# Causal attention on one Trainium2 core: transposes one step later, other score banks, maxima in two parts

## The reference

```python
def _temporal_experts(xt, idx, qw, qb, kw, kb, vw, vb, pw, pb):
    q = (jnp.einsum('btd,bod->bto', xt, qw[idx]) + qb[idx][:, None, :]).reshape(B, T, H, HD)
    k = ...
    v = ...
    logits = jnp.einsum('bthd,bshd->bhts', q, k) * HD ** (-0.5)
    causal = jnp.tril(jnp.ones((T, T), dtype=bool))
    logits = jnp.where(causal, logits, -jnp.inf)
    att = jax.nn.softmax(logits, axis=-1)
    o = jnp.einsum('bhts,bshd->bthd', att, v).reshape(B, T, D)
```

## Time and profile before

| what | us |
|---|---|
| median of 3 runs | 3260.94 (3252.55 to 3263.05) |
| the profiled execution's own time | 3263.12 |
| its span, first to last instruction | 3261.4 |
| the units of the causal attention, first to last exponential | 1883.96 to 2117.31 |
| TensorE busy in the span | 2921.0 |
| VectorE busy | 2001.2 |
| ScalarE busy | 1520.2 |

### The profile page before, as it was taken

One profiled execution on the slowest core, in us unless ns is written; L12 is line 12 of the kernel. 1 busy time (PEld: TensorE's weight loads), 2 busy tenths in 40 slices (PEclk: granted clock), 3 DMA queues, 4 the chain that ended last, 5 costly groups with the idle time before them and its releaser, 6 DMA issues. The chain is left out here.

```text
span 3261.4 us, 48231 instructions
## 1 busy us (share of the span) xinstructions
PE 2921.0 (90%) x15718; PEld 2067.5 (63%) x15718; DVE 2001.2 (61%) x4063; ACT 1520.2 (47%) x3320; POOL 945.4 (29%) x994
## 2 busy tenths in 40 slices
PE   5988699999689968799997989889999899998899
PEld 2622187776557645355555856568777687776787
DVE  6888736776521136799995256644777447776444
ACT  2500035666135526577774355524666346664322
POOL 2067573671134430677760000000000000001210
PEclk9999999999689989899998999999999999999999
DMA  3057755332669954555431653146220263201422
GB/s 98 17 166 203 200 151 131 64 66 50 178 226 335 336 154 148 184 147 161 147 106 42 199 131 82 25 135 171 60 56 22 64 190 80 59 22 40 113 78 84
DMA packets 227364, 401.31 MB, mean 123 GB/s; under 512 B 44750, under 2 KB 141154, under 8 KB 224942
## 3 DMA queue, kind: packets, MB, share of 16 engines
q1 hardware_dynamic: 176066, 260.74, 28.3%
q0 software_dynamic: 49744, 134.92, 14.9%
q10 hardware_dynamic: 1308, 2.56, 0.3%
HBM read 314.40 MB, written 87.71 MB: 123 GB/s over the span
## 5 line engine op out<-in xcount | busy, mean ns | idle before, releaser
L905 ACT ACTIVATE at_p<-at_pb,at_max 125x1250 f32<-125x1250 f32 (+4 forms) x320 | 383.8, 1199 | 301.9 <-DVE at_unused L976 273.3
L791 PE MATMUL at_pb<-ident,at_p 125*125 125x125 f32 x2880 | 431.9, 280 | 20.5 <-ACT at_p L905 17.7
L791 PEld LDWEIGHTS at_pb<-ident,at_p 125*125 125x125 f32 x2880 | 389.3, 190 | 83.3 <-ACT at_p L905 22.1
L808 PE MATMUL at_pb<-at_pt,at_v 125*64 125x250 f32 x2880 | 355.3, 383 | 5.2 <-DVE s_t L1009 3.0
L969 DVE TENSOR_REDUCE at_wide<-at_pb 125x1 f32<-125x1024 f32 x240 | 293.6, 1223 | 20.3 <-PE at_pb L774 2.0
L891 ACT ACTIVATE at_pt<-at_pb 125x500 f32<-125x500 f32 (+1 forms) x448 | 232.8, 520 | 94.8 <-PE at_pb L791 90.4
L808 PEld LDWEIGHTS at_pb<-at_pt,at_v 125*64 125x64 f32 x2880 | 188.4, 137 | 103.9 <-issue 14.3
L751 PE MATMUL at_pb<-at_s,at_shared 128*128 128x500 f32 (+1 forms) x1152 | 229.0, 361 | 22.9 <-ACT at_shared L853 22.9
L987 DVE COPY at_pt<-at_pb 125x500 f32<-125x500 f32 (+1 forms) x416 | 232.1, 582 | 21.9 <-PE at_pb L791 21.9
L976 DVE TENSOR_SCALAR_CACHE_REDUCE at_unused<-at_pb,at_wide 125x226 bf16<-125x226 f32 x240 | 107.7, 449 | 205.2 <-PE at_pb L774 202.3
L713 POOL TENSOR_TENSOR s_t<-s_t,at_all 128x500 f32<-128x500 f32 (+1 forms) x33 | 42.8, 1296 | 651.5 <-DVE s_t L1009 651.4
(11 more groups left out here) (340 smaller groups left out, 5694.1 us busy)
## 6 DMA issues: line engine op xcount, KB each, us to landing
w_ring<-in_L_ffn_w SPq DMA_DIRECT2D x128, 512.0 KB, 12.4
at_shared<-k_parts SPq DMA_DIRECT2D x64, 312.5 KB
ml_w<-in_mlp_w SPq DMA_DIRECT2D x64, 256.0 KB
k_parts<-at_shared SPq DMA_DIRECT2D x64, 250.0 KB, 2.8
q_parts<-at_shared SPq DMA_DIRECT2D x64, 250.0 KB, 2.8
h_edges<-em_both SPq DMA_DIRECT2D x44, 256.0 KB, 2.3
g_h<-h_edges SPq DMA_DIRECT2D x10, 1024.0 KB, 6.0
at_shared<-q_parts SPq DMA_DIRECT2D x32, 312.5 KB
```

The source lines that it names most:

```text
L791: ins = pe.transpose(pturn[0:TN, g % 2, TN * (t % 4):TN * (t % 4) + TN], p[:, u % 2, TN * t:TN * t + TN], c.ident[0:TN, 0:TN])
L808: ins = pe.matmul(pout[side:side + 64, 0:2 * TN], v[:, t, 2 * j + h, :], p_t[:, q % 2, t, :], start=(t < 2), stop=(t >= keys[u] - 2))
L905: act.activation(p[:, t % 2, 0:w], score[t % 2][0:TN, 0:w], ACT.Exp, bias=neg_max[:, t:t + 1], accum_out=total[:, t:t + 1]).then_inc(exp_d ...
```

## The change

Only the causal attention changes; the other three keep their instructions and order.

- `lag`: transposes and takes of a unit move from step u+2 to step u+3. TensorE's step s now is turns(s-3) parts 0 and 1, then scores(s), the quarters of duo (s-5)//2, and part 2 of the turns among them; a duo of up to 4 key tiles is done in one go. The lower half's copy and the addition move from odd step 2q+5 to even step 2q+6. The loops run one step longer.
- `place` and `spans`: units of fewer than 10 key tiles ("short") write their scores to banks of their own, even units to the first banks (`score[0]`), odd units to `apart`, the fourth and fifth bank, both in pieces that begin at column 0.
- The wait of a piece for the exponential of the unit before is left only in the third piece, where this unit and the one before are both full.
- Full units take the maximum in two parts. Even: `wide_max` over columns 0 to 1000, then `tail_max` masks 250 columns and takes the maximum over these. Odd: `wide_max` masks its last 125 columns and takes 1024, then `tail_max` takes the other 226.

```diff
--- before.py
+++ after.py
@@ -595,10 +595,16 @@
         keys = [(i // 2 * 2 + 2 if causal else NT) for _, _, i in units]
         turns = [-(-n // 4) for n in keys]
         upto = lambda u: sum(turns[:u])
+        full = lambda u: keys[u] == NT
+        wides = [u for u in range(NU) if causal and full(u)]
+        apart = flat[:, 3 * 512:5 * 512]
+        place = lambda u: apart if causal and u % 2 and not full(u) else score[u % 2]
+        spans = lambda u: pieces[0] if causal and not full(u) else pieces[u % 2]
+        lag = 3 if causal else 2
 
         taken = [(u, n) for u in range(NU) for n in range(turns[u])]
         by_act = lambda u, n: (n == 0 or (n == 2 and u % 2 == 0)) if causal else (n == 2) == (u % 2 == 0)
-        sum_at = lambda s: (s - 5) // 2 if causal and s % 2 == 1 else (s - 6) // 2 if not causal and s % 2 == 0 else -1
+        sum_at = lambda s: (s - 6) // 2 if s % 2 == 0 else -1
         act_by = lambda g: sum(1 for u, n in taken[:g] if by_act(u, n))
         dve_by = lambda g: g - act_by(g)
 
@@ -759,23 +765,23 @@
                     if u % UNITS == 0 and n == 0 and j >= 1:
                         pe.wait_ge(kq_in[j % 2], 16 * LOADS * ((j + 1) // 2))
                     w = TN * keys[u]
-                    there = [(a, min(b, w)) for a, b in pieces[u % 2] if a < w]
+                    there = [(a, min(b, w)) for a, b in spans(u) if a < w]
                     if n >= len(there):
                         return
                     a, b = there[n]
                     if u >= 2 and n == 0:
 
                         pe.wait_ge(exp_done, u - 1)
-                    if u >= 1 and a == (0 if u % 2 else 1024):
+                    if u >= 1 and full(u) and full(u - 1) and n == 2:
 
                         pe.wait_ge(exp_done, u)
-                    pe.matmul(score[u % 2][0:TN, a:b], q_two[j % 2][h][:, TN * i:TN * i + TN], k_hi[j % 2][h][:, a:b],
+                    pe.matmul(place(u)[0:TN, a:b], q_two[j % 2][h][:, TN * i:TN * i + TN], k_hi[j % 2][h][:, a:b],
                               start=True, stop=False)
-                    ins = pe.matmul(score[u % 2][0:TN, a:b], q_two[j % 2][h][:, TN * i:TN * i + TN], k_lo[j % 2][h][:, a:b],
+                    ins = pe.matmul(place(u)[0:TN, a:b], q_two[j % 2][h][:, TN * i:TN * i + TN], k_lo[j % 2][h][:, a:b],
                                     start=False, stop=True)
                     if n == len(there) - 1:
                         ins.then_inc(scored, 1)
-                    elif n == 1 and not causal:
+                    elif n == 1:
                         ins.then_inc(wide_scored, 1)
 
                 def turn_part(u, n):
@@ -812,19 +818,28 @@
 
                 pe.wait_ge(first_in, 16 * LOADS)
                 pe.wait_ge(low, len(items) - 3)
-                for s in range(NU + 4):
+                for s in range(NU + 5 if causal else NU + 4):
                     if s == 2:
 
                         pe.wait_ge(low, len(items))
                     if causal:
-                        quarter = 2 * (s % 2)
-                        turn_part(s - 2, 0)
+                        q, at = (s - 5) // 2, 2 * ((s - 5) % 2)
+                        short = 0 <= q < NU // 2 and keys[2 * q] <= 4
+                        wide = s < NU and full(s)
+                        turn_part(s - lag, 0)
+                        turn_part(s - lag, 1)
                         score_part(s, 0)
-                        turn_part(s - 2, 1)
-                        duo_sum((s - 4) // 2, quarter, quarter + 1)
-                        score_part(s, 1)
-                        turn_part(s - 2, 2)
-                        duo_sum((s - 4) // 2, quarter + 1, quarter + 2)
+                        if wide:
+                            score_part(s, 1)
+                        if not short:
+                            duo_sum(q, at, at + 1)
+                        turn_part(s - lag, 2)
+                        if not wide:
+                            score_part(s, 1)
+                        if not short:
+                            duo_sum(q, at + 1, at + 2)
+                        elif at == 0:
+                            duo_sum(q, 0, 4)
                         score_part(s, 2)
                     elif s % 2 == 0:
                         turn_part(s - 2, 0)
@@ -893,8 +908,8 @@
                                    ACT.Copy).then_inc(act_took, 1)
 
                 act.wait_ge(w_low, len(parts))
-                for s in range(NU + 4 if causal else NU + 5):
-                    take_part(s - 2, 0)
+                for s in range(NU + 5):
+                    take_part(s - lag, 0)
                     if 1 <= s <= NU:
                         t = s - 1
                         act.wait_ge(max_ready, t + 1)
@@ -902,10 +917,10 @@
 
                             act.wait_ge(turned, upto(t - 1))
                         w = TN * keys[t]
-                        act.activation(p[:, t % 2, 0:w], score[t % 2][0:TN, 0:w], ACT.Exp,
+                        act.activation(p[:, t % 2, 0:w], place(t)[0:TN, 0:w], ACT.Exp,
                                        bias=neg_max[:, t:t + 1], accum_out=total[:, t:t + 1]).then_inc(exp_done, 1)
-                    take_part(s - 2, 1)
-                    take_part(s - 2, 2)
+                    take_part(s - lag, 1)
+                    take_part(s - lag, 2)
                     if sum_at(s) >= 0:
                         q = sum_at(s)
                         act.wait_ge(pv_done, q + 1)
@@ -953,27 +968,44 @@
 
                 if save is not None:
                     dve.wait_ge(saved, 16)
+                def mask(u):
+                    w, m = TN * keys[u], TN * (2 - u % 2)
+                    late = place(u)[0:TN, w - m:w]
+                    dve.tensor_tensor(late, late, c.causal[:, 0:m], ALU.add).then_inc(masked, 1)
+                    dve.wait_ge(masked, u + 1)
+
                 def whole_max(u):
                     w = TN * keys[u]
                     dve.wait_ge(scored, u + 1)
-                    m = TN * (2 - u % 2)
-                    late = score[u % 2][0:TN, w - m:w]
-                    dve.tensor_tensor(late, late, c.causal[:, 0:m], ALU.add).then_inc(masked, 1)
-                    dve.wait_ge(masked, u + 1)
-                    dve.tensor_reduce(neg_max[:, u:u + 1], score[u % 2][0:TN, 0:w], AX, ALU.max, negate=True)\
+                    mask(u)
+                    dve.tensor_reduce(neg_max[:, u:u + 1], place(u)[0:TN, 0:w], AX, ALU.max, negate=True)\
                         .then_inc(max_ready, 1)
 
                 def wide_max(u):
                     a = pieces[u % 2][0][0]
-                    dve.wait_ge(wide_scored, u + 1)
-                    dve.tensor_reduce(neg_wide[:, u:u + 1], score[u % 2][0:TN, a:a + 1024], AX, ALU.max, negate=True)\
+                    b = a + 1024
+                    if causal:
+                        dve.wait_ge(wide_scored, wides.index(u) + 1)
+                        if u % 2:
+                            mask(u)
+                        else:
+                            b = N - 2 * TN
+                    else:
+                        dve.wait_ge(wide_scored, u + 1)
+                    dve.tensor_reduce(neg_wide[:, u:u + 1], score[u % 2][0:TN, a:b], AX, ALU.max, negate=True)\
                         .then_inc(wide_ready, 1)
 
                 def tail_max(u):
-                    a = pieces[u % 2][2][0]
+                    a, b = pieces[u % 2][2]
                     dve.wait_ge(scored, u + 1)
-                    dve.wait_ge(wide_ready, u + 1)
-                    dve.tensor_scalar(unused[:, 0:TAIL], score[u % 2][0:TN, a:a + TAIL], -1.0, neg_wide[:, u:u + 1],
+                    if causal:
+                        dve.wait_ge(wide_ready, wides.index(u) + 1)
+                        if u % 2 == 0:
+                            mask(u)
+                            a = N - 2 * TN
+                    else:
+                        dve.wait_ge(wide_ready, u + 1)
+                    dve.tensor_scalar(unused[:, 0:b - a], score[u % 2][0:TN, a:b], -1.0, neg_wide[:, u:u + 1],
                                       ALU.mult, ALU.min, accum_out=neg_max[:, u:u + 1]).then_inc(max_ready, 1)
 
                 def take_part(u, n):
@@ -987,13 +1019,13 @@
                     dve.tensor_copy(p_t[:, u // 2 % 2, 4 * n:4 * n + m, TN * (u % 2):TN * (u % 2) + TN],
                                     pturn[0:TN, g % 2, 0:TN * m].rearrange("p (a b) -> p a b", b=TN)).then_inc(dve_took, 1)
 
-                for s in range(NU + 4 if causal else NU + 5):
+                for s in range(NU + 5):
                     if 1 <= s <= NU:
-                        (whole_max if causal else tail_max)(s - 1)
-                    u = s - 2
+                        (tail_max if full(s - 1) else whole_max)(s - 1)
+                    u = s - lag
                     take_part(u, 0)
                     take_part(u, 1)
-                    if not causal and s < NU:
```

(1 more changed line is left out.)

## The result

The changed kernel takes 3240.09 us (median, 3230.24 to 3244.23) against 3262.43 (3252.55 to 3265.78) of the kernel before in the same comparison: a ratio of 0.9932 with a 95% interval of 0.9915 to 0.9949, 22 us faster. Forecast: 3240, range 3226 to 3256.

The account below looks back on a forecast made before the run. Rings of waits, not one full engine, set the pace. A pair falls from 60.41 us to 54.8, net 20.5 saved: 3263.1 profiled becomes 3242.6, and as that execution stood 2.2 above the median, 3240; range 3226 to 3256.

Parts of the forecast that it names:

- Ring A: Per duo, exponential, lower half's copy, addition, mask, maximum, next exponential: 3.50 us before with 8 key tiles, 3.65 forecast.
- Even to odd: Exponential of an even short unit to the next odd unit's: 1.34 us with 4 key tiles, 1.55, 1.8 to 2.1.
- signs of being wrong: Listed signs: full units at 3.0, the group of 4 key tiles above 10, TensorE without gaps with 8.
- The new wait: Exponentials wait for transposes of the unit two before, behind scores and PV; seen at units 18, 19 and 1.
- 16 to 19: Full units of 10 key tiles, exponential 16 to 19: forecast 11.9 us against 11.86, so not shorter.
- The maximum in two parts: Full units: maximum after the last piece shrinks from 1.46 to about 0.55 us; VectorE spends 0.3 more a unit.
- 19 to 4: From unit 19's exponential to the next pair's unit 4: forecast 13.5 us against 13.05.
- Half clock: TensorE at its lower clock behind light units of 2 key tiles: 0.7 us added a pair, 0.4 in the first.
- The rival that saw TensorE lose more to the lower clock: Low clock falls on units of 6 or 8 key tiles, 3.5 us a pair, time 3254 (3250 to 3258); 20%.
- The end: Last exponential to the reciprocal: from 4.36 to 6.2 us, two units' transposes still to come, a loss of 1.9.
- The sum: Savings of 6.7 us in the first pair, 5.6, 5.0 and 5.0 in the others, less 1.9: net 20.5.
- 8 to 12: Group of units with 6 key tiles, exponential 8 to 12: forecast 9.7 us against 10.96.

Follow-up runs that it names:

- copy_twice: Changed kernel with ScalarE copying the lower half of each duo out twice in the causal attention; 3249.3 us, ratio 0.9966 to the kernel before.
- no_lag: Changed kernel with transposes, takes, PV and addition a step earlier again, and the old order within TensorE's step; 3257.1 us, ratio 0.9986 to the kernel before.
- part2_early: Changed kernel with part 2 of the transposes issued right behind the first score piece, ahead of the second and of PV; 3229.8 us, ratio 0.9904.
- one_max: Changed kernel with one mask and one maximum over 1250 columns in full causal units; 3241.5 us, ratio 0.9939 to the kernel before.
- late_add: Changed kernel with VectorE's addition of a duo one place later, behind the next maximum; 3234.9 us, ratio 0.9934 to the kernel before.
- early_late: Changed kernel with part 2 of the transposes early and the addition behind the next maximum; 3231.3 us, ratio 0.9909 to the kernel before.
- best: Changed kernel with the addition behind the next maximum, and all transposes and the first two score pieces ahead of PV; 3221.5 us, ratio 0.9894.

## Why the prediction was right

- **Ring A stays, the other half shrinks.** Right, in direction and size. Ring A was read from the earlier trace rows and carried over with 0.15 for the mask: 3.65 forecast, 3.68 measured with 8 key tiles, 3.18 and 3.17 with 6, 2.71 and 2.69 with 4. Even to odd: 1.34, 1.55, 1.8 to 2.1 forecast; 0.93 and 1.14, 1.34 and 1.50, 1.76 and 2.06 measured. The smaller ones were too long because both terms, exponential 0.79 and take 0.55, were a tenth too long from start to start. They are 0.67 and 0.47 here, between units 6 and 7:

```profile
1946.96 0.68 ACT L920 ACTIVATE at_p<-at_pb,at_max 125x500 f32<-125x500 f32 x1 [0.91 <-DVE at_max L981]
...
1947.63 0.58 ACT L906 ACTIVATE at_pt<-at_pb 125x500 f32<-125x500 f32 x1
...
1948.10 0.68 ACT L920 ACTIVATE at_p<-at_pb,at_max 125x500 f32<-125x500 f32 x1
```

From 4 to 5 (0.93) the take is also narrower, that of a unit of 2 key tiles. copy_twice shows that the ring is closed, no_lag that the lag, with its order of TensorE's work, is what took ScalarE's wait for transposes away. One of the prediction's signs of being wrong did appear, TensorE without gaps in the group of 8; copy_twice, where ring A grows and TensorE again shows no gap, says that the sign was a bad one: a gapless row of matmuls does not show that TensorE sets the pace.
- **The new wait at the full units.** Right: it appears at units 18 and 19 and at the next pair's 0 and 1, and 16 to 19 did not get shorter (11.9 forecast, 12.14). Term by term: 16 to 17 is 2.95, not 2.65; 17 to 18 5.07, not 5.4; 18 to 19 4.12, not 3.85. The errors nearly cancel. part2_early shows the wait and its price, 1.6 us a pair in these units.
- **The maximum in two parts pays for the wait.** Right in kind, as one_max shows: 1.36 us a pair, at units 16 and 17 alone. By count of operations it should have cost 0.3 a unit; VectorE does spend that: from unit 12 to 19 of the second pair it is busy 17.95 us with the split (9.04 and 8.91) and 16.74 in one_max (8.83 and 7.91), 1.2 us for four units. But it does so ahead of the last piece, where nobody waits.
- **19 to 4.** 13.5 forecast, 13.76 measured. The five single intervals missed by up to 0.4: 3.2, 3.1, 2.3, 1.0 and 3.9 forecast; 3.53, 3.31, 2.23, 1.17 and 3.52 measured.
- **Half clock.** The term of 0.7 a pair was wrong: it is 0 in pairs two to four, and in the first pair, where 0.4 stood in the sum, it is 1.2. The changed kernel's stretch of light units in the third pair, by the windows view, against the earlier trace rows:

```profile
1988.00:1995.00 7.00, 6.57 (x49) 4.01 (x48) 2.96 (x8) 3.29 (x10) 0.00 (x0) 1.00 0.04 1
```

The granted clock is 1.00, that is 2.4 GHz, and it stays there in pairs two to four; before, each had a stretch at the lower level. In the first pair the changed kernel had the lower level too. Its units 4 to 8 there, and those of one_max, whose instructions are the same in this stretch:

```profile
1888.29:1897.16 8.87, 8.10 (x44) 5.30 (x44) 4.99 (x11) 5.64 (x14) 0.00 (x0) 0.88 1.05 275
...
1878.23:1885.94 7.71, 6.71 (x41) 4.65 (x40) 4.87 (x11) 5.54 (x15) 0.00 (x0) 1.00 1.04 275
```

The transfers are alike, the clock is not (0.88 and 1.00), and 1.16 us lie between them. So part of what the lag seemed to win between units 4 and 8 (11.24, 10.72 and 10.67 before in pairs two to four, 9.63 in the first at 0.98) is the clock: 1.6, 1.1 and 1.0 us, 3.7 in all, less the 1.2 that the changed kernel lost in its first pair. By this estimate some 2.5 of the 22.8 us below are the clock. no_lag bears this out, with 10.68 for that group in the second and 10.67 in the third pair, 9.60 in the fourth. Its windows view over 13 us from unit 2 on, in the third and the fourth pair:

```profile
2003.00:2016.00 13.00, 10.16 (x48) 6.21 (x44) 5.63 (x13) 6.72 (x19) 0.73 (x1) 0.74 0.87 185
2061.00:2074.00 13.00, 8.56 (x53) 4.91 (x50) 6.84 (x16) 7.37 (x20) 0.73 (x1) 1.00 0.30 91
```

The clock differs (0.74 and 1.00), and so does the load of the transfers (0.87 and 0.30 of the DMA engines). That the transfers are not the cause, two groups of units 4 to 8 show: the kernel before took 10.67 in its fourth pair at a DMA share of 0.06 and a clock of 0.84, and the changed kernel takes 7.70 at a share of 1.03 in the second pair and of 0.41 in the fourth, both at 1.00. The rival that saw TensorE lose more to the lower clock went the wrong way in pairs two to four.
- **The end.** A loss of 1.9 was forecast; exponential to reciprocal is 6.86, was 4.36, a loss of 2.5. For the reciprocal:

```profile
2097.81 0.17 DVE L1035 RECIPROCAL at_inv<-at_sum 125x4 f32<-125x4 f32 x1
```

The transfers behind it took 6.47 us to the last operation instead of 7.60, which no edit explains.
- **The sum.** From the first exponential to the reciprocal, 237.71 us became 214.95: 22.8. Forecast 20.5. That the span fell by nearly the same, 22.7, is chance: the first exponential also came 1.1 earlier and the transfers behind the reciprocal were 1.1 shorter, and 2.3 were lost behind them. Pairs two to four won 6.5, 6.0 and 6.2 against 5.6, 5.0 and 5.0 (the clock term, 0.2 of sums, and in the last pair 0.2 more, as no pair follows it), the first 6.5 against 6.7, the end lost 0.6 more.

That the forecast of 3240 and the median agree to 0.1 us is luck: the medians carry several us, and the profiled span moved by 22.7, not 20.5. What can be claimed is the table of groups.

Left open: what holds 8 to 12 at 9.3 us in every kernel in which ring A is open (TensorE busy 0.87 of it in late_add and early_late, 0.92 in best). The rows under best point to PV of a whole duo ahead of the transposes; no run put it back in quarters there, so that is read and not tested.

## What to carry to other kernels

When engines are idle and the waits view names each of them, look for the ring: add the rows from one instruction back to itself, and see whether the sum is the distance between two of its starts. A ring that the edit leaves in place can be carried over to the new kernel with its few changed rows, and this gave each group here within 0.5 us. Don't take an engine's gapless row for the bound: lengthen the ring by a known amount, as copy_twice does, and see who follows. Moving work a step later frees one wait only together with the buffers for it (here, without its own banks the lag made the kernel slower), and it lands in front of another user of a shared buffer: look up where in the engine's list that work stands, and put it there as early as its inputs are ready.

## What the runs showed of the hardware

Two things I had not expected. The granted clock of TensorE stayed at its upper level through the light units of pairs two to four, where it had fallen in each of these pairs before. In the kernel before, TensorE had been busy 8.93 of the 11 us ahead of the fall at 2011; in the changed one, which carries transposes of full units one step further into the light ones, 6.57 of the 7 us from 1988. The windows view of the kernel before:

```profile
2000.00:2011.00 11.00, 8.93 (x62) 5.21 (x61) 5.01 (x13) 4.97 (x16) 0.72 (x1) 1.00 0.33 72
```

That the denser work kept the clock up is argued from these rows; no run varied it by itself, and there is more to it: in no_lag TensorE is busy 10.3 of 12.4 us from unit 19 to the next unit 4 in each of the last three pairs, and the clock fell behind it in two of them and stayed up in the third. The other: at the same clock the distances between exponentials repeat within some 0.03 us from pair to pair and over kernels whose first exponential differs by 10 us in time (in the last pair, which no other follows, a few differ by up to 0.3), so a change of 0.3 us a pair can be read from one trace where medians of 3240 us can't tell 5.
